# State-space scan and quantized feed-forward on one core: two additions of x begun behind the scan's last product, and a second early row quantized by DVE

## Chip, cores and metric

The kernel runs on one core of a Trainium2 chip (trn2). The metric is the device time of one execution in microseconds (us). Engines: PE multiplies matrices, DVE, ACT and POOL work on vectors, SP only issues DMAs here. POOL issues DMAs too; they run on a queue of their own, q0 (software), those of SP on q1 (hardware).

## What is computed

Cut to what matters, with the inputs x (4, 512, 512) and ctx (4, 512, 256):

```
z = layernorm(x)
u = silu(causal_conv(in_proj(ctx)) + conv_b);  B, C, dt = x_proj(u);  delta = softplus(dt_proj(dt) + b)
for each time step t:  state = state * exp(delta_t * A) + delta_t * u_t * B_t
                       y_t = sum over the 16 state columns n of state[:, n] * C_t[n]
x = x + (y + D * u) * silu(z)
h = silu(bit_linear(layernorm(x), w_gate)) * bit_linear(layernorm(x), w_up)
x = x + bit_linear(rms_norm(h) * ln_w, w_down)
```

bit_linear rounds its weights to −1, 0, 1 and each row of its input to 8 bits, with a scale from the row's largest magnitude.

## The kernel before

**Front.** Projections, convolution, softplus, the layernorm of x, its transpose and silu, the transpose of delta * u, and the rounding of the weights for gate and up (stored in HBM as w_ternary). All of x's memory on the chip (x_all, 16 rows of 128 x 512, four for each batch) then holds silu(z).

**Scan.** 64 steps, k = 16 * b + n, for batch b = 0 to 3 (a block of 16 steps each) and state column n. In a step ACT makes dB (L665, or a diagonal matrix, L662) and dA (four exponentials, L669), PE turns dB into four PSUM banks (L1182, or L1179 for the six columns of DIAG), DVE runs four scans of 128 x 512 (L882, which the profile lists as TENSOR_TENSOR_SCAN), POOL multiplies the four results by a row of C, laid over all partitions (L466, `product`), and PE adds the product up in four other PSUM banks, transposed (L1195, `add`; L1207 adds D * u in steps 4 to 7 of a block). PE's order is written out: in step k it turns dB for step k + 2, piece by piece between the four adds of product k − 1. The scans' results have a ring of four buffers (hs), so DVE may be three steps ahead of POOL. The rows of C come from HBM (c_rows) through SP's queue, one for each step (L334, `load_c`), each issued when the product two steps earlier is done, since c_bc has two buffers. After a batch's last step DVE multiplies its sum with silu(z) (`gate_y`, L892, four of 128 x 512), two scans into the third step of the next block; for batch 3, behind the scan. `add_x(b)` (L474) then adds x itself: a DMA from HBM, issued by POOL, that adds 1 MB into the batch's four rows of x_all.

SP's queue also carries in the scan: the rounded weights for gate (block 1) and up (block 2), w_down's raw pieces and ln_w (block 3) (L261, L345).

**Early rows in block 3.** The feed-forward part works by tiles t = 0 to 15 of 128 rows. Tile t needs the rows' statistics on DVE (`variance`, `bias`, L898 to L915), the reciprocal root on POOL (`power`, L478), the normalization on ACT (`norm`, L650), the row's scale on DVE (`scale_row`), the rounding on ACT, and the last step, the subtraction of MAGIC and the limit to 127, to bf16: `q1(t)`, 128 x 512. Then SP turns it by a DMA transpose into q1T (`turn_q1`, L349), which PE reads. For tiles 0 to 2 (EARLY) this is done within the scan's last block; POOL does the last step for tiles 0 and 1 (L492, behind products 6 and 10 of the block), DVE that for tile 2 behind its last scan (`cut_x`, L953).

**Behind the scan.** DVE waits for POOL's product of step 62 and makes the last one itself in two halves (L988), then cut_x(2), gated_up(0, 0) (L970) and gate_y(3). PE: the adds of step 62, gate_and_up(0, 0), the adds of step 63, gate_and_up(0, 1), and from then on the units of eight matmuls gate_and_up(t, j) for j = 0 to 3 (L1229), each first one of a tile waiting for q1T of the tile, and `down` for tile t − 2 at j = 2 (L1236). Each unit runs through ACT's silu (L714), DVE's gated_up (L970) and POOL's weighing with ln_w (L500). DVE's first statistics of batch 1 (`variance(4)`) come in tile 1, between gated_up(1, 0) and gated_up(1, 1); they wait for add_x(1). Those of batch 2 come in tile 5 and those of batch 3 in tile 9.

Of the kernel before, what the change touches and what calls it, by code (L numbers as in the profile page):

```python
# [25 lines left out]
ALU = mybir.AluOpType  # L26
# [4 lines left out]
NB, L, E = 4, 512, 512  # L31
# [13 lines left out]
MAGIC = 1.5 * 2.0 ** 23  # L45
# [22 lines left out]
def mixer_ffn(nc, x, ctx_t, in_t, conv_w, conv_b, xp_t, dt_t, dt_b, a_log, d_skip, w_all, ln_w, out):  # L68
    es = ExitStack()
    with es:  # L70
# [3 lines left out]
        def sem(name):  # L74
            return es.enter_context(nc.semaphore(name))
# [11 lines left out]
        def gate_rows(b):  # L87
            return x_all[:, b * KL:(b + 1) * KL, :]
# [94 lines left out]
        S = {n: sem(n) for n in names}  # L183
# [18 lines left out]
        def hold(eng, *waits):  # L202

            for name, v in zip(waits[0::2], waits[1::2]):
                if v > 0:
                    eng.wait_ge(S[name] if isinstance(name, str) else name, v)
# [33 lines left out]
        def xn(t):  # L240
            return xn_early[:, t, :] if t < EARLY else xn_late[:, t % 2, :]

        def q1(t):
            return (q1_early if t < EARLY else q1_late)[:, t % EARLY, :]

        def added(k, half):

            if k % DS == DS - 1 and half == 1:
                return "y_done", (k // DS + 1) * KL
            return "p_added", k * 2 + half + 1 - k // DS  # L250
# [8 lines left out]
        def _(sp):  # L259
            def load(dst, src, s):  # L260
                sp.dma_start(dst, src).then_inc(S[s], 16)  # L261
# [69 lines left out]
            def load_c(k):  # L331
                s, n = k % 2, k // 2
                hold(sp, "p_ready", k - 1)
                sp.dma_start(c_bc[:, s, :], c_dram[k // DS, k % DS, :].partition_broadcast(P)  # L334
                             ).then_inc(c_loaded[s], 16)
# [4 lines left out]
            def load_ternary(dst, w, k, s):  # L340
                sp.wait_ge(wq_stored[w][k], 16)
                load(dst[:, k, :], wq_dram[w * 4 + k, :, :], s)

            def load_down(k):
                sp.dma_start(w_full(WD_AT[k]), w_all[8 + k, :, :]).then_inc(wd_loaded[k], 16)  # L345

            def turn_q1(t):
                sp.wait_ge(S["q1_ready"], t + 1)
                sp.dma_start(q1T[:, t, :, :], q1(t), transpose=True).then_inc(q1T_done[t], 16)  # L349
# [7 lines left out]
            for b in range(NB):  # L357
                for n in range(DS):
                    if b * DS + n > 1:
                        load_c(b * DS + n)  # L360
                    if n >= 4 and n % 2 == 0 and n < 12 and b > 0:
                        k = n // 2 - 2
                        sp.wait_ge(S["y_gated"], b * KL)
                        if b == 1:
                            load_ternary(wg, 0, k, "wg_loaded")
                        if b == 2:
                            load_ternary(wu, 1, k, "wu_loaded")
                        if b == 3 and k < 2:
                            load_down(k)
                        if b == 3 and k == 2:  # L370
                            load(lnw, ln_w.partition_broadcast(P), "lnw_loaded")
                    if b == 3 and n == 12:
                        hold(sp, *added(b * DS + 8, 0))
                        load_down(3)
                    if b == 3 and n in (9, 13):
                        turn_q1(n // 4 - 2)
            sp.wait_ge(S["dA_ready"], NB * DS * KE)
            load_down(2)

            def store_out(t):  # L380
# [3 lines left out]
                    sp.wait_ge(S["fin_done"], t + 1)  # L384
                sp.dma_start(out_v[:, t, :], o_s[:, t % 2, :]).then_inc(out_stored[t % 2], 16)

            turn_q1(2)
            for t in range(TILES + 3):
                if tile(t - 3):
# [10 lines left out]
        def _(pool):  # L400
# [61 lines left out]
            def product(k):  # L462
                s = k % 2
                pool.wait_ge(c_loaded[s], (k // 2 + 1) * 16)
                pool.wait_ge(S["scan_done"], k * KE + KE)
                nc.gpsimd.tensor_tensor(hs[:, k % RING, :, :], hs[:, k % RING, :, :],  # L466
                                        c_bc[:, s:s + 1, :].to_broadcast([P, KE, L]),
                                        ALU.mult).then_inc(S["p_ready"], 1)
# [3 lines left out]
            def add_x(b):  # L472
                pool.wait_ge(S["y_gated"], (b + 1) * KL)
                nc.gpsimd.dma_start(gate_rows(b), x_v[:, b, :, :], accum_op=ALU.add).then_inc(x1_added[b], 16)  # L474

            def power(n, first, last):
                hold(pool, "var_ready", n)
                nc.gpsimd.tensor_tensor(rstd2[:, first:last], var2[:, first:last], mhalf[:, first:last],  # L478
                                        ALU.pow).then_inc(S["rstd_ready"], 1)

            for b in range(NB):
                for n in range(DS):
                    if b * DS + n < LAST:
                        product(b * DS + n)
                    if n == 3 and b > 0:
                        add_x(b - 1)
                    if b == NB - 1 and n % 4 == 0 and n // 4 < EARLY:
                        power(n // 4 + 1, 0, 1)
                    if b == NB - 1 and n in (6, 10):
                        t = n // 4 - 1  # L490
                        pool.wait_ge(S["x_rounded"], t + 1)
                        nc.gpsimd.tensor_scalar(q1(t), xn(t), MAGIC, 127.0, ALU.subtract,  # L492
                                                ALU.min).then_inc(S["q1_ready"], 1)
            add_x(NB - 1)

            def weigh(t, s, half):

# [271 lines left out]
        def _(dve):  # L769
# [179 lines left out]
            def cut_x(t):  # L949
                dve.wait_ge(S["x_rounded"], t + 1)  # L950
                if t >= 2 * EARLY:
                    dve.wait_ge(q1T_done[t - EARLY], 16)
                nc.vector.tensor_scalar(q1(t), xn(t), MAGIC, 127.0, ALU.subtract, ALU.min).then_inc(S["q1_ready"], 1)  # L953
# [13 lines left out]
            def gated_up(t, j):  # L967
                dve.wait_ge(S["sg_ready"], t * 4 + j + 1)
                dve.wait_ge(S["u_psum"], t * 4 + j + 1)
                nc.vector.tensor_tensor(h2[:, t % 2, j * 512:(j + 1) * 512], sg[:, j % 2, :], ps[:, U_BANK[(t * 4 + j) % 3], :],  # L970
                                        ALU.mult).then_inc(S["h_ready"], 1)

            for b in range(NB):
                for n in range(DS):
                    scan(b * DS + n)
                    t = n // 4
# [9 lines left out]
            for half in range(2):  # L986
                rows = slice(2 * half, 2 * half + 2)
                nc.vector.tensor_tensor(hs[:, LAST % RING, rows, :], hs[:, LAST % RING, rows, :],  # L988
                                        c_bc[:, LAST % 2:LAST % 2 + 1, :].to_broadcast([P, 2, L]),
                                        ALU.mult).then_inc(S["p_last"], 1)  # L990
            cut_x(2)
            gated_up(0, 0)
            gate_y(NB - 1)
# [315 lines left out]
```

## Time and profile before

| | us |
|---|---|
| median of three runs | 599.01 (597.3 to 599.84) |
| profiled execution, its own time | 597.98 |
| span of its trace | 596.2 |
| PE busy | 543.2 (91%) |
| DVE busy | 538.6 (90%) |
| ACT busy | 516.2 (87%) |
| POOL busy | 464.3 (78%) |

The span runs from the first instruction's start to the last one's end. Busy times are unions over each engine's instructions; waiting and the issuing of DMAs by SP are not counted. The scan's steps lie between about 100 and 414 us of the span, the feed-forward part behind them. In the timelines a row merges neighbouring instructions of one line: start, length, engine, line, operation, operands, how many, and in brackets how long the engine idled ahead of it and who ended that.

### The profile page before, as it was taken

To read this page: it belongs to the slowest core of one execution; us is meant where nothing else is said; L and a number is where in the kernel's file an instruction comes from. 1 tells how busy PE (TensorE), PEld (TensorE's weight loads), DVE (VectorE), ACT (ScalarE), POOL (GpSimd) and SP (SyncE) were. 2 spreads that over 40 slices of the span, in tenths; PEclk is the share of its full clock that TensorE was granted. 3 is DMA by queue.
4 is the path that set the end of the run, shared out by engine and by line. 5 is a ranking of instruction groups with operands and counts; after the bars stand their busy time and mean duration, and the time that the engine had idled before them with its cause. 6 is when DMAs were issued, how large, how long until landed. Compare 5 with 4: busy or idle time off the path is not lost.

```text
span 596.2 us, 10170 instructions
## 1 busy us (share of the span) xinstructions
PE 543.2 (91%) x3613; PEld 404.8 (68%) x3630; DVE 538.6 (90%) x814; ACT 516.2 (87%) x754; POOL 464.3 (78%) x182
## 2 busy tenths in 40 slices
PE   5977975799999999999899889998988999998996
PEld 2422565799998999989899889987333444443442
DVE  2999676999999999999999999998899999999874
ACT  2998698999999999989999798999877778867774
POOL 3574784799998999999899999994666565665662
PEclk9996788999999999999999899999999999999999
DMA  8993462111221652115531166243444342534421
GB/s 295 410 366 104 152 233 85 31 59 54 58 68 55 130 153 90 54 62 129 151 103 56 54 159 197 96 128 103 72 88 81 78 108 62 107 80 83 100 58 53
DMA packets 63185, 68.63 MB, mean 115 GB/s; under 512 B 42144, under 2 KB 42144, under 8 KB 60960
## 3 DMA queue, kind: packets, MB, share of 16 engines
q1 hardware_dynamic: 60832, 63.63, 36.0%
q0 software_dynamic: 2304, 4.36, 4.4%
q8 instruction: 29, 0.48, 0.3%
q14 instruction: 20, 0.16, 0.1%
HBM read 50.02 MB, written 8.52 MB: 98 GB/s over the span
## 4 chain that ended last, share of the span: by engine, by line
PE 27%; DVE 23%; ACT 21%; POOL 12%; issue 10%; DMA 6%; SPq 0%; DVEq 0%; ACTq 0%; POOLq 0%
POOL arena L466 11%; ACT arena L669 9%; ACT arena L665 7%; PE ps L1195 6%; DVE arena L792 5%; PE ps L1179 5%; PE ps L1229 4%; PE ps L1236 3%; PE ps L1182 3%; DVE arena L882 3%; DVE arena L970 2%; PE ps L1095 2%; DMA arena<-arena 2%; DMA arena<-c_rows 2%; ACT arena L662 2%
## 5 line engine op out<-in xcount | busy, mean ns | idle before, releaser
L466 POOL TENSOR_TENSOR arena<-arena 128x2048 f32<-128x2048 f32 x63 | 286.7, 4606 | 18.0 <-DVE arena L882 15.0
L882 DVE TENSOR_TENSOR_SCAN arena<-arena,ps 128x512 f32<-128x512 f32 x256 | 287.3, 1197 | 7.0 <-PE ps L1182 4.3
L669 ACT ACTIVATE arena<-arena,a_neg 128x512 f32<-128x512 f32 x256 | 165.1, 710 | 9.0 <-DVE arena L882 8.9
L1195 PE MATMUL ps<-ident,arena 128*128 128x128 f32 x1024 | 155.9, 276 | 7.0 <-POOL arena L466 3.8
L1195 PEld LDWEIGHTS ps<-ident,arena 128*128 128x128 f32 x1024 | 120.7, 142 | 11.2 <-POOL arena L466 7.0
L500 POOL TENSOR_TENSOR arena<-arena 128x1024 f32<-128x1024 f32 x30 | 71.1, 2372 | 58.2 <-DVE arena L970 58.2
L1229 PE MATMUL ps<-arena 128*128 128x512 bf16 x504 | 112.9, 379 | 2.1 <-DVE arena L970 1.1
L1182 PE MATMUL ps<-ident,arena 128*128 128x128 f32 x640 | 98.4, 279 | 10.1 <-ACT arena L665 7.8
L1179 PE MATMUL ps<-arena 128*128 128x128 f32 x768 | 103.4, 279 | 2.4 <-ACT arena L665 2.3
L665 ACT ACTIVATE arena<-arena,bT 128x512 f32<-128x512 f32 x160 | 101.9, 708 | 4.0 <-DVE a_neg L872 2.6
L1179 PEld LDWEIGHTS ps<-arena 128*128 128x128 f32 x768 | 94.9, 195 | 4.0 <-ACT arena L665 2.5
L1229 PEld LDWEIGHTS ps<-arena 128*128 128x128 bf16 x512 | 49.9, 98 | 62.4 <-DVE arena L970 2.1
L1182 PEld LDWEIGHTS ps<-ident,arena 128*128 128x128 f32 x640 | 76.2, 144 | 13.3 <-issue 8.5
L1236 PE MATMUL ps<-arena 128*128 128x512 bf16 x247 | 57.1, 379 | 8.1 <-DMA arena<-arena 5.5
L741 ACT ACTIVATE arena<-arena,magic,aq 128x2048 f32<-128x2048 f32 x15 | 31.4, 2093 | 29.5 <-DVE aq L931 29.4
L1236 PEld LDWEIGHTS ps<-arena 128*128 128x128 bf16 x256 | 24.3, 98 | 39.3 <-DMA arena<-arena 9.5
L714 ACT ACTIVATE arena<-ps,scales 128x512 f32<-128x512 f32 x64 | 42.6, 680 | 7.3 <-PE ps L1229 7.2
L970 DVE TENSOR_TENSOR arena<-arena,ps 128x512 f32<-128x512 f32 x64 | 43.5, 679 | 3.6 <-PE ps L1229 3.1
L1069 PE MATMUL ps<-arena 128*128 128x512 f32 x64 | 30.7, 638 | 9.8 <-DMA arena<-in_t 6.6
L957 DVE TENSOR_REDUCE half_max<-arena 128x1 f32<-128x1024 f32 x30 | 36.5, 1216 | 2.3
L436 POOL TENSOR_SCALAR arena<-arena,mv_x,rstd_x 128x512 f32<-128x512 f32 x16 | 34.0, 2132 | 0.4
L792 DVE SCALAR_TENSOR_TENSOR arena<-ps,cw,arena 128x511 f32<-128x511 f32 (+2 forms) x48 | 31.7, 736 | 0.0
(116 smaller groups left out, 576.5 us busy)
## 6 DMA issues: line engine op xcount, KB each, us to landing
arena<-w_all SPq DMA_DIRECT2D x16, 1024.0 KB, 9.4
arena<-c_rows SPq DMA_DIRECT2D x64, 256.0 KB, 3.3
arena<-x SPq DMA_DIRECT2D x4, 1024.0 KB, 18.0
w_ternary<-arena SPq DMA_DIRECT2D x8, 512.0 KB, 3.5
arena<-w_ternary SPq DMA_DIRECT2D x8, 512.0 KB, 5.1
arena<-x POOLq DMA_DIRECT2D x4, 1024.0 KB, 9.9
out<-arena SPq DMA_DIRECT2D x16, 256.0 KB, 2.0
arena<-ctx_t SPq DMA_DIRECT2D x4, 512.0 KB, 12.2
```

What stands on the lines that cost most here:

```text
L466: nc.gpsimd.tensor_tensor(hs[:, k % RING, :, :], hs[:, k % RING, :, :], c_bc[:, s:s + 1, :].to_broadcast([P, KE, L]), ALU.mult).then_inc(S ...
L500: nc.gpsimd.tensor_tensor(p2[:, s, w], h2[:, s, w], lnw[:, w], ALU.mult).then_inc(S["p2_ready"], 1)
L665: nc.scalar.activation(dB[:, slot(k), i, :], turned[:, b, i, :], ACT.Copy, scale=bT[:, b, i, n:n + 1]).then_inc(S["dB_ready"], 1)
L669: nc.scalar.activation(dA[:, s, i, :], delta_u[:, b, 0, i, :], ACT.Exp, scale=a_neg[:, i, n:n + 1]).then_inc(S["dA_ready"], 1)
L792: nc.vector.scalar_tensor_tensor(out=v[:, k, i:], in0=two("conv", b, h)[:, j, 0:L - i], scalar=cw[:, k, TAPS - 1 - i:TAPS - i], in1=v[:, k ...
L882: nc.vector.tensor_tensor_scan(out=hs[:, k % RING, i, :], data0=dA[:, k % 2, i, :], data1=ps[:, 4 + i, :], initial=0.0, op0=ALU.mult, op1= ...
L970: nc.vector.tensor_tensor(h2[:, t % 2, j * 512:(j + 1) * 512], sg[:, j % 2, :], ps[:, U_BANK[(t * 4 + j) % 3], :], ALU.mult).then_inc(S["h ...
L1179: last = mm(to, turned[:, k // DS, c, i * P:(i + 1) * P], dgB[:, slot(k), c, :], start=True, stop=True)
L1182: last = nc.tensor.transpose(to, dB[:, slot(k), c, i * P:(i + 1) * P], ident[:])
L1195: last = mm(ps[:, c, i * P:(i + 1) * P], hs[:, k % RING, i, c * P:(c + 1) * P], ident[:], start=(n == 0 and i == 0), stop=(n == DS - 1), i ...
L1229: last = mm(ps[:, bank, :], q1T[:, t, c, :], w[:, c, j * 512:(j + 1) * 512], start=(c == 0), stop=(c == KE - 1))
L1236: last = mm(ps[:, DOWN_BANK[t % 2], :], q2T[:, t % 2, c, :], wd(c), start=(c == 0), stop=(c == KI - 1))
```

## The change

Additions: add_x(0) stays in the scan, behind product 3 of block 1. add_x(1), add_x(2) and add_x(3) are issued by POOL one after the other behind its last product; before, the first two stood behind product 3 of blocks 2 and 3. Tile 1's last step of quantization goes from POOL (behind product 10 of block 3) to DVE (behind the last product, ahead of tile 2's). The DMA transpose of tile 1 goes in SP's list from behind the row of C of step 61 to the place behind the load of w_down's last piece, ahead of tile 2's.

```diff
@@ SP
-                    if b == 3 and n in (9, 13):
-                        turn_q1(n // 4 - 2)
+                    if b == 3 and n == 9:
+                        turn_q1(0)
             sp.wait_ge(S["dA_ready"], NB * DS * KE)
             load_down(2)
@@
+            turn_q1(1)
             turn_q1(2)
             for t in range(TILES + 3):
@@ POOL
-                    if n == 3 and b > 0:
-                        add_x(b - 1)
+                    if n == 3 and b == 1:
+                        add_x(0)
                     if b == NB - 1 and n % 4 == 0 and n // 4 < EARLY:
                         power(n // 4 + 1, 0, 1)
-                    if b == NB - 1 and n in (6, 10):
-                        t = n // 4 - 1
-                        pool.wait_ge(S["x_rounded"], t + 1)
-                        nc.gpsimd.tensor_scalar(q1(t), xn(t), MAGIC, 127.0, ALU.subtract,
+                    if b == NB - 1 and n == 6:
+                        pool.wait_ge(S["x_rounded"], 1)
+                        nc.gpsimd.tensor_scalar(q1(0), xn(0), MAGIC, 127.0, ALU.subtract,
                                                 ALU.min).then_inc(S["q1_ready"], 1)
-            add_x(NB - 1)
+            for b in range(1, NB):
+                add_x(b)
@@ DVE
+            cut_x(1)
             cut_x(2)
             gated_up(0, 0)
             gate_y(NB - 1)
```

POOL's list from block 3 of the scan (the products are L466 before, L467 in the changed file; the additions are the DMAs) to the first weighing of the feed-forward part, before:

```order
L466 TENSOR_TENSOR arena<-arena 128x2048 x3
L474 DMA arena<-x 128x4x512
L466 TENSOR_TENSOR arena<-arena 128x2048
L478 TENSOR_TENSOR rstd<-var,mhalf 128x1
L466 TENSOR_TENSOR arena<-arena 128x2048 x2
L492 TENSOR_SCALAR arena<-arena 128x512
L466 TENSOR_TENSOR arena<-arena 128x2048 x2
L478 TENSOR_TENSOR rstd<-var,mhalf 128x1
L466 TENSOR_TENSOR arena<-arena 128x2048 x2
L492 TENSOR_SCALAR arena<-arena 128x512
L466 TENSOR_TENSOR arena<-arena 128x2048 x4
L474 DMA arena<-x 128x4x512
```

and now:

```order
L467 TENSOR_TENSOR arena<-arena 128x2048 x4
L479 TENSOR_TENSOR rstd<-var,mhalf 128x1
L467 TENSOR_TENSOR arena<-arena 128x2048 x2
L492 TENSOR_SCALAR arena<-arena 128x512
L467 TENSOR_TENSOR arena<-arena 128x2048 x2
L479 TENSOR_TENSOR rstd<-var,mhalf 128x1
L467 TENSOR_TENSOR arena<-arena 128x2048 x6
L475 DMA arena<-x 128x4x512 x3
```

Three additions stand together behind the last product, one of the two quantizations of POOL is gone, and six products follow each other at the end.

SP's list at the end of the scan (rows of C L334, w_down's pieces L345, the transposes to q1T L349, the first one to q2T L354), before:

```order
L345 DMA arena<-w_all 128x2048
L334 DMA arena<-c_rows 128x512
L349 DMA_TRANSPOSE arena<-arena 128x4x128
L334 DMA arena<-c_rows 128x512 x2
L345 DMA arena<-w_all 128x2048
L349 DMA_TRANSPOSE arena<-arena 128x4x128
L354 DMA_TRANSPOSE arena<-arena 128x16x128
```

and now:

```order
L345 DMA arena<-w_all 128x2048
L334 DMA arena<-c_rows 128x512 x3
L345 DMA arena<-w_all 128x2048
L349 DMA_TRANSPOSE arena<-arena 128x4x128 x2
L354 DMA_TRANSPOSE arena<-arena 128x16x128
```

Tile 1's transpose now stands with tile 2's, behind the last rows of C and the last piece of w_down.

## Rows read from the trace of the kernel before

**Rows 1.** Windows: busy us of PE, PEld, DVE, ACT, POOL; clock, DMA share, GB/s.
```profile
190.00:265.00 75.00, 73.52 (x649) 71.23 (x648) 74.83 (x70) 72.65 (x131) 72.42 (x17) 1.00 0.37 99
265.00:340.00 75.00, 71.46 (x631) 69.31 (x629) 73.70 (x71) 71.28 (x128) 73.11 (x19) 1.00 0.37 99
...
479.40:490.00 10.60, 10.41 (x48) 4.81 (x50) 9.99 (x27) 8.38 (x10) 6.61 (x5) 1.00 0.39 88
```
**Rows 2.** Timeline of DVE, the scans of the second and the third block.
```profile
189.16 71.62 DVE L882 TENSOR_TENSOR_SCAN arena<-arena,ps 128x512 f32<-128x512 f32 x64
...
263.25 30.10 DVE L882 TENSOR_TENSOR_SCAN arena<-arena,ps 128x512 f32<-128x512 f32 x27
293.70 7.97 DVE L882 TENSOR_TENSOR_SCAN arena<-arena,ps 128x512 f32<-128x512 f32 x7 [0.35 <-PE ps L1182]
301.98 27.43 DVE L882 TENSOR_TENSOR_SCAN arena<-arena,ps 128x512 f32<-128x512 f32 x24 [0.30 <-PE ps L1179]
```
**Rows 3.** Timeline of POOL, second and third block.
```profile
212.09 63.43 POOL L466 TENSOR_TENSOR arena<-arena 128x2048 f32<-128x2048 f32 x14 [0.91 <-DMA arena<-c_rows]
275.43 1.24 POOL L474 DMA_DIRECT2D arena<-x  x1
276.27 9.49 POOL L466 TENSOR_TENSOR arena<-arena 128x2048 f32<-128x2048 f32 x2
287.66 49.76 POOL L466 TENSOR_TENSOR arena<-arena 128x2048 f32<-128x2048 f32 x11 [1.89 <-DMA arena<-c_rows]
```
**Rows 4.** What PE waited for, 264 to 330 us.
```profile
PE ps L1195 <- POOL arena L466: 1.8, 1, 1.8
```
**Rows 5.** Timeline of DVE, the scan's end and tiles 0 and 1.
```profile
397.17 11.20 DVE L882 TENSOR_TENSOR_SCAN arena<-arena,ps 128x512 f32<-128x512 f32 x10
409.34 2.36 DVE L988 TENSOR_TENSOR arena<-arena 128x1024 f32<-128x1024 f32 x2 [0.98 <-POOL arena L466]
411.62 0.42 DVE L953 TENSOR_SCALAR arena<-arena 128x512 bf16<-128x512 f32 x1
413.12 0.69 DVE L970 TENSOR_TENSOR arena<-arena,ps 128x512 f32<-128x512 f32 x1 [1.08 <-PE ps L1229]
...
422.71 0.68 DVE L970 TENSOR_TENSOR arena<-arena,ps 128x512 f32<-128x512 f32 x1
423.30 0.69 DVE L898 BATCH_NORM_STATS2 bst<-arena 128x6 f32<-128x512 f32 x1
```
**Rows 6.** Timeline of POOL, the scan's end.
```profile
389.17 1.93 POOL L492 TENSOR_SCALAR arena<-arena 128x512 bf16<-128x512 f32 x1
391.18 18.09 POOL L466 TENSOR_TENSOR arena<-arena 128x2048 f32<-128x2048 f32 x4
417.25 1.34 POOL L474 DMA_DIRECT2D arena<-x  x1 [7.98 <-DVE arena L892]
```
**Rows 7.** The 15 loads of rows of C between 112 and 180 us.
```profile
DMA to landing us min/median/max: 3.0/3.2/3.4
```
**Rows 8.** The chain that ended last, 281 to 288 us.
```profile
281.28 6.31 DMA arena<-c_rows
```
**Rows 9.** DMA view of 205 to 209 us: queues, and what SP issued.
```profile
q0 software_dynamic: 365, 0.75, 105.6%
...
arena<-c_rows SPq DMA_DIRECT2D x1, 256.0 KB, 5.3
```
**Rows 10.** The four additions, from issue to landing.
```profile
DMA to landing us min/median/max: 9.0/9.9/11.8
```
**Rows 11.** SP's transpose of tile 2, and how long it took to land.
```profile
412.07 1.20 SPq L349 DMA_TRANSPOSE arena<-arena  x1
...
DMA to landing us min/median/max: 2.4/2.4/2.4
```
**Rows 12.** Timeline of PE, units from gate_and_up(0, 2) on.
```profile
417.01 12.26 PE L1229 MATMUL ps<-arena 128*128 128x512 bf16 x55 [0.52 <-DVE arena L892]
```
**Rows 13.** DMA queues, 6.5 to 10.5 us, at the kernel's start.
```profile
q1 hardware_dynamic: 500, 1.22, 92.6%
q0 software_dynamic: 169, 0.16, 14.9%
```

## The prediction

> **What bounds the kernel now.** I read the timeline of DVE first, then POOL's, then the waits of PE, and last the DMA views, because the change moves transfers and hardly any arithmetic.
>
> Within the scan three engines are full: over 75 us of the second block PE is busy 73.5 us, DVE 74.8 and POOL 72.4 [rows 1]. DVE sets the pace. Where nothing disturbs it, ten scans take 11.20 us [rows 5]: the next begins 1.112 us after the last, and one step (four scans) takes 4.45 us. POOL's product takes about 4.53 us a step (14 in 63.43 us [rows 3]), so POOL drifts behind DVE by 0.08 us a step, which costs nothing until PE, which adds a product only when POOL has made it, comes too late with DVE's next input. DVE's timeline shows where that happens. From 263.25 to 329.41 (the end of the last piece, 301.98 + 27.43) it runs 58 scans; at 1.112 each and with the 0.08 us by which a scan outlasts its slot that is 64.6 us, and it took 66.2: **1.6 us lost**, the visible waits being for PE [rows 2]. The second block (64 scans in 71.62 us) lost only 0.4 by the same sum.
>
> Why there? POOL issues batch 1's addition at 275.43 (1.24 us of POOL), its next two products take 9.49 us (two undisturbed ones 9.06), and then POOL idles 1.89 us for a row of C that a DMA brings [rows 3]. PE in turn waits 1.8 us for POOL's product, the only wait of PE that this view lists [rows 4]. The row of C took 6.3 us from issue to landing, where 15 earlier ones took 3.0 to 3.4 [rows 7, 8]. The DMA view of 205 to 209 us, the same place one block earlier, says why: the software queue q0, which carries the addition, moves 365 packets at a share of 105.6%, and SP's queue q1 not one, though a row of C was issued at that time [rows 9]. **An addition, once at full rate, keeps SP's transfers out altogether.** This is the reading on which both the gain and the loss below rest.
>
> **The change part by part**, against the profiled execution (span 596.2, time 597.98; the median of the three runs is 599.01, 1.03 above it; I put the difference on the median).
>
> *Addition of batch 1 out of the third block.* Removes from POOL about 1.24 us of issue and slowed products, and the 1.89 us wait. PE then has its product some 3 us earlier and the 1.6 us of DVE should go. Below, 0 (PE is itself busy 71.5 of 75 us in the third block [rows 1] and might stall DVE anyway); above, 1.6. The second block, where POOL lagged less, lost 0.4, so I take 1.6 as the third's gain: with no addition at all it should lag less than the second did. What is late next is DVE itself.
>
> *Addition of batch 2 out of the fourth block.* Nothing: DVE there carries the rows' statistics besides its scans, so POOL catches up with it at every chain of them.
>
> *POOL's quantization of row 1.* 1.93 us off POOL, four products ahead of the end. POOL's last product ends at 409.27 (391.18 + 18.09) [rows 6] and DVE idles 0.98 us for it before its own last product [rows 5]. The scans of that product's step ended at 403.92 (408.37 less four slots); a product that starts 0.2 after that and takes 4.57 ends at 408.7. Gain 0.6; bounds 0 and 0.98. Both gains: **2.2 us**.
>
> *cut_x(1) on DVE.* 0.42 us more [rows 5], ahead of an idle time of 1.08 us that PE ends. Hidden; without that cover 0.42.
>
> *Two more issues on POOL behind its last product.* POOL idled 7.98 us there for DVE's gate [rows 6], so 2.6 us of issuing is hidden, and the addition of batch 3 is still issued 8.0 us after the last product (417.25). Variance(4), DVE's first reader of batch 1, comes 14.0 us after the last product (423.30 [rows 5]); additions landed after 9.0 to 11.8 us [rows 10], so it doesn't wait.
>
> *What these issues do to SP's queue.* Before, the transpose of row 2 went out at 412.07 into idle DMA engines and landed in 2.4 us [rows 11]; row 1's had been done in the scan. Now rows 1 and 2 are both turned there. I count from POOL's last product (409.27 before). The transpose of row 1 goes out at +2.8, as row 2's did. The addition of batch 1, issued at 0, is by then at full rate and batch 2's is queued behind it. PE needs row 1 at +11.2: its run of seven units from 417.01 takes 12.26 us, 1.75 each, and row 1 is the third [rows 12]. Its landing isn't in the trace, so I bound it. Below: as before, 2.4 after issue, +5.2, no loss. Above: behind all three additions. One lands 9.0 after its issue at best [rows 10]; each further one adds its bytes at the rate of [rows 9], 1.05 MB (four tiles of 128 x 512 floats) at 0.75 MB in 4 us, 5.6 us. So the three end at +9.0, +14.6 and +20.2, and a transfer that was kept out lands 0.4 us or a little more after (C's row at 281.28 + 6.31 = 287.59, its addition at 275.43 + 11.8 = 287.2 [rows 3, 8, 10]). I take **the middle case**, order of arrival: the first two additions are issued at 0 and +1.3, ahead of the transpose (+2.8), the third at +8, behind it. So row 1 lands behind the second, +15.2. PE is then 4.0 us late. DVE's product of row 1 started 0.45 us after PE's unit ended (422.71 against 420.51 + 1.75), so 3.5 us reach DVE. Behind it wait everything of DVE's list, variance(4) among it, ACT's silu(1, 0) and POOL's weighing of row 1; the feed-forward part then runs at DVE's pace (busy 9.99 of 10.6 us of a tile, PE 10.41 [rows 1]), so nothing is made good. Row 2 is needed six units in, at +18.2, now +22.2, and even behind the third addition (+20.8) it is in time.
>
> Sum: −2.2 + 3.5 = +1.3: **600.3 us**.
>
> **The rivals.**
>
> *1. SP's transposes get a turn between the additions.* For it: an addition is one transfer of its own, so the lock-out may hold for one only; in the kernel's first microseconds the two queues shared the engines well, q0 14.9% beside q1 92.6% [rows 13]. Against it: the full lock-out of [rows 9], with no second addition queued. Row 1 then lands at about +9.6 (9.0 and the same 0.6 as above), within the 11.2. Time 599.01 − 2.2 = **596.8 us**. The Trainium skill (DMA: Bandwidth & Descriptors, "Queues, rings and completion order") says that a DMA engine takes turns between its queues packet by packet, a packet having 9 to 17 descriptors as a rule and at most 64. By that rule this rival is what happens; the trace agrees with it at the start and not within one addition.
>
> *2. They wait for all three.* The engines stay with q0 as long as it has work, and the third addition, issued at +8, is queued before the second ends (+14.6). Row 1 lands at +20.8, PE is 9.6 late, DVE 9.1: +6.9 net, **605.9 us**, slower. It decides as soon as q0 is never empty from 0 to +20. For it: not a packet of q1 in the four microseconds of [rows 9]; against: no trace of two additions in a row.
>
> *3. The change doesn't give what it says:* the third block's stall is PE's own load (71.5 of 75 us [rows 1]) and stays, and only 0.6 is gained. With the forecast's loss, **601.9 us**.
>
> **How the numbers follow.** Forecast 0.34, rival 1 0.27, rival 2 0.22, rival 3 0.08, and 0.09 for what I don't see, half each way. A measurement of this kernel can tell about 0.5%, 3 us: under 596.0 or over 602.0. Faster: a quarter of rival 1 and half the rest, 0.11. Slower: rival 2, half of rival 3, a fifth of the forecast, half the rest, 0.36. Same: 0.53. The range goes from a little under rival 1 to a little over rival 2, 595.6 to 606.8. The likeliest case's own range is 599 to 602.
>
> **What would show it.** The timeline of DVE in the third block: 58 scans in under 65 us instead of 66.2, and no wait of POOL for C; else the first gain is wrong. DVE's idle time before its last product: 0.4 or less instead of 0.98. The landing of row 1's transpose: 7 us after issue for rival 1, about 12 for the forecast, 18 for rival 2; and a wait of PE for a DMA before its third unit of the feed-forward part, none, 4 or 9.6 us. If DVE waits for an addition ahead of variance(4), the forecast is wrong in a way I have not priced.

## The result and the profile after

| | before | changed |
|---|---|---|
| median, us | 598.15 | 605.38 |
| lowest to highest, 6 runs each | 596.02 to 599.84 | 601.4 to 607.67 |
| profiled execution: time (span), us | 597.98 (596.2) | 607.67 (605.9) |
| mean granted TensorE clock in it | 0.968 | 0.961 |

The ratio on record, which is worked out from all six runs of each and differs a little from the quotient of the medians, is 1.0116, with a 95% interval of 1.0089 to 1.0143: slower, by 7.2 us between the medians. The profiled execution is the slowest of the six; its extra 9.7 us of span hold 1.46 us that were lost before the second block began (190.62 against 189.16), in a part that the change doesn't touch.

**The gain came as forecast.** DVE and then POOL in the changed kernel, second and third block (columns as in [rows 2] and [rows 3]):

```profile
190.62 71.59 DVE L883 TENSOR_TENSOR_SCAN arena<-arena,ps 128x512 f32<-128x512 f32 x64
262.27 2.48 DVE L893 TENSOR_TENSOR arena<-ps,arena 128x512 f32<-128x512 f32 x4
264.67 64.54 DVE L883 TENSOR_TENSOR_SCAN arena<-arena,ps 128x512 f32<-128x512 f32 x58
```
```profile
202.09 1.41 POOL L475 DMA_DIRECT2D arena<-x  x1
203.02 9.61 POOL L467 TENSOR_TENSOR arena<-arena 128x2048 f32<-128x2048 f32 x2
213.46 122.22 POOL L467 TENSOR_TENSOR arena<-arena 128x2048 f32<-128x2048 f32 x27 [0.82 <-DMA arena<-c_rows]
```

The third block's 58 scans took 64.54 us in one stretch where they took 66.16 [rows 2], and POOL made 27 products without a gap where it had waited 1.89 us for C [rows 3].

**At the scan's end** DVE, then PE (compare [rows 5] and [rows 12]):

```profile
394.71 13.44 DVE L883 TENSOR_TENSOR_SCAN arena<-arena,ps 128x512 f32<-128x512 f32 x12 [0.24 <-ACT arena L670]
409.19 2.36 DVE L989 TENSOR_TENSOR arena<-arena 128x1024 f32<-128x1024 f32 x2 [1.03 <-DMA arena<-c_rows]
411.46 0.76 DVE L954 TENSOR_SCALAR arena<-arena 128x512 bf16<-128x512 f32 x2
412.34 0.69 DVE L971 TENSOR_TENSOR arena<-arena,ps 128x512 f32<-128x512 f32 x1
...
420.69 1.22 DVE L958 TENSOR_REDUCE half_max<-arena 128x1 f32<-128x1024 f32 x1
431.47 0.69 DVE L971 TENSOR_TENSOR arena<-arena,ps 128x512 f32<-128x512 f32 x1 [9.55 <-PE ps L1231]
...
439.73 1.23 DVE L1020 TENSOR_SCALAR arena<-arena 128x2048 bf16<-128x2048 f32 x1 [0.84 <-ACT arena L742]
```
```profile
408.54 1.97 PE L1197 MATMUL ps<-ident,arena 128*128 128x128 f32 x16 [0.71 <-POOL arena L467]
...
416.23 3.63 PE L1231 MATMUL ps<-arena 128*128 128x512 bf16 x16 [0.53 <-DVE arena L893]
427.77 13.38 PE L1231 MATMUL ps<-arena 128*128 128x512 bf16 x48 [7.91 <-DMA arena<-arena]
```

Up to 420.69 everything is ahead of before: there DVE's maximum of row 0 began at 421.57, so 0.88 us are gained in spite of the 1.46 lost at the front, 2.3 in all. Then PE, two units into its run of seven, stops for 7.91 us for a DMA, and DVE's product of row 1 begins at 431.47 instead of 422.71 [rows 5]. The loss at this place is 8.76 + 0.88 = **9.64 us**. Nothing is made good behind it, and 0.9 us more is lost before the tile is through, where DVE waits 0.84 us for ACT's rounding (439.73): the first transpose of the feed-forward part proper goes out at 440.99 instead of 431.35, 9.64 us late, and the last one 9.71 us. The sum for the profiled execution is 1.46 − 2.3 + 9.6 + 0.9 = 9.7 us, its whole difference of span. Without the front's 1.46 it is 8.2, beside 7.2 of the medians (5.3 to 8.6 by the interval).

**What the DMA was.** SP's queue, and the source view of POOL's additions and of SP's transposes:

```profile
404.00 0.32 SPq L334 DMA_DIRECT2D arena<-c_rows  x1
404.37 0.43 SPq L345 DMA_DIRECT2D arena<-w_all  x1
411.91 4.43 SPq L349 DMA_TRANSPOSE arena<-arena  x2
440.99 1.84 SPq L354 DMA_TRANSPOSE arena<-arena  x1
```
```profile
L475 POOL DMA_DIRECT2D arena<-x x3: 1283/1335/1775, 408.4 to 416.5; - x3
DMA to landing us min/median/max: 9.9/15.8/18.2
```
```profile
L349 SPq DMA_TRANSPOSE arena<-arena x3: 1777/1780/2610, 411.9 to 442.9; - x3
DMA to landing us min/median/max: 3.0/15.7/15.8
```

In order of issue: addition 1 at 408.42 landed at 418.29; addition 2 at 409.30, landed 425.13; the transposes of tiles 1 and 2 at 411.91 and 413.73 landed at 427.72 and 429.42; addition 3 at 416.47, landed 434.65. POOL's last product ended at 408.49, so the transpose of tile 1 landed at **+19.2**, where +11.2 was needed and +15.2 forecast.

Two DMA views of the changed kernel show how the queues shared the engines meanwhile (columns: packets, MB, share of 16 engines). A packet of these views is called a record here. From 411.5 to 415.5 us, with a transpose issued at 411.91:

```profile
q0 software_dynamic: 381, 0.78, 109.2%
```

and from 414 to 430 us:

```profile
q0 software_dynamic: 1320, 2.61, 93.0%
q1 hardware_dynamic: 1088, 0.26, 14.4%
```

In the first, SP's queue q1 isn't listed: it moved nothing, as in [rows 9]. In the second it moved 1088 records, both transposes, among 1320 of q0. Taken in bins of 0.5 us the records show three phases: up to 415.9, while the first addition drains, q0 alone; from 416 to 428 about as many records of q1 as of q0, some 45 each; then what is left. A data record of q0 is 2 KB and takes 178 ns, one of q1 256 bytes and 32 ns. One for one, the transposes' 545 records each pass only as fast as 545 of q0's do, some 6 us, though by itself such a transpose takes 2.4 us [rows 11].

That explains a landing near 422.5 to 424.4, and not the whole of it. Each DMA here signals its end in 16 parts, and the trace has their times. Of tile 1's transpose 15 parts came between 423.02 and 424.42 (+15.9), and the last one only at **427.72**, 3.3 us later. PE waits for the last. Of the third addition, too, 15 parts came from 429.00 to 429.75 and the last at 434.65.

**The clock.** Windows of the changed kernel around the wait (columns as in [rows 1]):

```profile
416.00:424.00 8.00, 3.63 (x16) 1.49 (x16) 4.52 (x9) 3.52 (x4) 6.53 (x4) 0.96 1.17 192
424.00:434.00 10.00, 6.23 (x16) 2.24 (x17) 2.32 (x7) 3.26 (x4) 0.48 (x1) 0.52 0.59 99
434.00:442.00 8.00, 7.20 (x35) 3.09 (x33) 6.77 (x20) 6.86 (x7) 2.61 (x3) 1.00 0.00 0
```

PE ran to 419.86, idled, and from 423.32 had the 1.2 GHz level for 10.2 us, so it came back to work with half the clock. Its first unit took 3.6 us, not 1.75: of the 9.64 lost, 7.9 are the wait itself, and the rest is this.

### The profile page after: what moved, and what is told of

Same layout as the page of the kernel before. It is cut to its first block, busy times and chain, and to the rows that moved or that the text cites. A ratio compares the mean times of both kernels' runs of the same rounds, so it can differ in the third digit from the quotient of the medians.

```text
span 605.9 us, 10187 instructions
## 1 busy us (share of the span) xinstructions
PE 547.0 (90%) x3630; PEld 404.9 (67%) x3630; DVE 539.4 (89%) x815; ACT 515.9 (85%) x754; POOL 462.4 (76%) x181
## 4 chain that ended last, share of the span: by engine, by line
PE 37%; DVE 24%; ACT 17%; issue 8%; DMA 8%; POOL 5%; SPq 0%; DVEq 0%; ACTq 0%; POOLq 0%
PE ps L1197 9%; ACT arena L670 8%; PE ps L1181 7%; PE ps L1231 6%; PE ps L1184 5%; ACT arena L666 5%; DVE arena L793 5%; DMA arena<-arena 5%; DVE arena L883 5%; POOL arena L467 4%; PE ps L1238 4%; DVE arena L971 2%; PE ps L1097 2%; DMA arena<-c_rows 2%; DMA arena<-x 1%
## 5 line engine op out<-in xcount | busy, mean ns | idle before, releaser
L467 POOL TENSOR_TENSOR arena<-arena 128x2048 f32<-128x2048 f32 x63 | 286.0, 4589 | 20.6 <-DVE arena L883 18.4
L1231 PE MATMUL ps<-arena 128*128 128x512 bf16 x512 | 116.5, 386 | 9.2 <-DMA arena<-arena 7.9
L1238 PE MATMUL ps<-arena 128*128 128x512 bf16 x256 | 58.0, 379 | 7.3 <-DMA arena<-arena 5.3
```

The lines of the kernel that those rows point to most:

```text
L1231: last = mm(ps[:, bank, :], q1T[:, t, c, :], w[:, c, j * 512:(j + 1) * 512], start=(c == 0), stop=(c == KE - 1))
L1238: last = mm(ps[:, DOWN_BANK[t % 2], :], q2T[:, t % 2, c, :], wd(c), start=(c == 0), stop=(c == KI - 1))
```

## The experiments

All were run against the kernel before, in two sets; its medians were 597.35 (31 runs) and 597.29 (24 runs). The ratios are those on record; where the effect is small they lie up to 0.15% below the quotients of the medians, so the sizes of the small gains are known no better than that. The edits are shown against the changed kernel. "+x" is microseconds after POOL's last product, which to 0.1 us is when its first addition there is issued.

**additions_only: the three additions moved, row 1 left with POOL and turned in the scan.**

```
-                    if b == 3 and n == 9:
-                        turn_q1(0)
+                    if b == 3 and n in (9, 13):
+                        turn_q1(n // 4 - 2)
...
-            turn_q1(1)
...
-                    if b == NB - 1 and n == 6:
+                    if b == NB - 1 and n in (6, 10):
...
-            cut_x(1)
```

> Theory A: the loss is tile 1's transpose, which waits on SP's queue behind the additions. Here the three additions stand behind the last product as in the change, but tile 1 is quantized by POOL and turned within the scan as before. The third block of the scan gains the 1.6 us, tile 1 finds its rows turned, and only tile 2's transpose goes beside the additions; it lands 15 to 19 us after POOL's last product and is needed at +18.2. So 0 to 1 us of loss and 1.5 to 2.2 of gain: 596 to 598 against 598.15. Theory B: the loss lies in the additions themselves (x of batch 1 late for variance(4), or POOL busy with descriptors). Then nothing of the 7 us goes: about 605, and DVE idles ahead of variance(4).

Measured 596.16 (594.83 to 598.63, 10 runs), ratio 0.9975 (0.9949 to 1.0002). PE's run of seven units is unbroken:

```profile
416.64 12.26 PE L1230 MATMUL ps<-arena 128*128 128x512 bf16 x55 [0.53 <-DVE arena L893]
```

The third block's 58 scans took 64.55 us. The additions still queued up (408.82 to 418.77, 409.71 to 424.43, 416.88 to 430.24), and tile 2's transpose, issued at 412.44, took 11.4 us, landing at +15.0, but it is needed only at +18:

```profile
DMA to landing us min/median/max: 11.4/11.4/11.4
```

So the additions by themselves cost nothing there; what costs is that a transpose is needed early behind them.

**row1_only: row 1 on DVE and turned behind the scan; the additions as before.**

```
-                    if n == 3 and b == 1:
-                        add_x(0)
+                    if n == 3 and b > 0:
+                        add_x(b - 1)
...
-            for b in range(1, NB):
-                add_x(b)
+            add_x(NB - 1)
```

> The other half alone: additions as before, tile 1 quantized by DVE behind the scan and turned there. Theory A: both transposes go into idle DMA engines and land within 6 us of POOL's last product, 5 us before PE needs the first. The 0.6 us at the scan's end stay, the third block keeps its stall: 597.0 to 598.2. Theory C: two transposes in a row on SP's queue, each issued in 1.8 to 2.6 us, are slow by themselves; then PE waits for tile 1 here too and the time is 601 or more.

Measured 597.99 (596.36 to 599.08), ratio 0.9999 (0.9972 to 1.0026). Both transposes went through idle engines, the first from 413.18 to 416.71 in 3.52 us, the second in 2.72, and PE waited for none. DVE's second quantization costs nothing, and neither half of the change is slow: **only the two together are**. The 0.6 us that this half should gain is too small to be told here.

**one_behind: batch 2's addition stays in the fourth block, batch 1's goes behind the last product.**

```
-                    if n == 3 and b == 1:
-                        add_x(0)
+                    if n == 3 and b in (1, 3):
+                        add_x(b - 1)
...
-            for b in range(1, NB):
-                add_x(b)
+            add_x(1)
+            add_x(NB - 1)
```

> As the change, but batch 2's addition stays in the scan's last block as before; only batch 1's stands behind the last product, and batch 3's follows at +8 as in both kernels. Theory A: tile 1's transpose waits for one addition and lands at +9.5 to +11, in time for PE at +11.2; the whole gain of 2.2 us shows: 595.5 to 597.5. If a single addition already makes it late, PE waits 1 to 3 us and the time is 597 to 599.

Measured **595.82** (594.12 to 597.64, 10 runs), ratio 0.9959 (0.9935 to 0.9983): the lowest median of all, 1.5 us under its set's kernel before by the medians and 2.4 by the ratio, though not told apart from in_block3 or additions_only. With a single addition ahead (407.58 to 417.40) tile 1's transpose was kept until it was nearly through and landed at 417.86, +10.3, within the +11.2:

```profile
410.99 3.88 SPq L349 DMA_TRANSPOSE arena<-arena  x2
```
```profile
415.38 12.26 PE L1231 MATMUL ps<-arena 128*128 128x512 bf16 x55 [0.53 <-DVE arena L893]
```

So it is the second addition, queued right behind the first, that makes tile 1 late.

**in_block3: batch 1's addition behind product 8 of the fourth block, batch 2's behind product 3.**

```
-                    if n == 3 and b == 1:
-                        add_x(0)
+                    if n == 3 and b in (1, 3):
+                        add_x(b - 1)
+                    if n == 8 and b == 3:
+                        add_x(1)
...
-            for b in range(1, NB):
-                add_x(b)
+            add_x(NB - 1)
```

> As the change, but batch 1's addition is issued in the scan's last block behind product 8, and batch 2's stays behind product 3 of it. DVE has its chains of small operations there, so POOL's lag should be made good and a late row of C be absorbed. Theory A: transposes in 6 us, no wait of PE, the third block without its stall: 595.5 to 597. If the additions stall the last block as they did the third, it is 597.5 to 598.5, with POOL waiting for a row of C around step 59 and DVE's scans stretched.

Measured 596.12 (594.82 to 598.0), ratio 0.9973 (0.9947 to 0.9999); the transposes took 2.45 and 2.78 us. POOL has room for two additions in the fourth block, as the part on batch 2's addition assumed. Its last product is then the last thing that DVE waits for, as before the change:

```profile
407.64 2.36 DVE L990 TENSOR_TENSOR arena<-arena 128x1024 f32<-128x1024 f32 x2 [1.28 <-POOL arena L467]
```

**third_later: the changed kernel with batch 3's addition moved to the end of tile 1**, so that nothing is queued behind the first two.

```
-            for b in range(1, NB):
+            for b in range(1, NB - 1):
                 add_x(b)
...
+                    if t == 1:
+                        add_x(NB - 1)
```

> As the change, but batch 3's addition is issued at the end of tile 1 instead of at +8 from POOL's last product, so only two additions are queued ahead of or beside the transposes. In the changed kernel's trace tile 1's transpose shared the DMA engines packet by packet with the second and third addition. If the third matters, tile 1 lands at +14 to +16 and the time is 600 to 602; if the second alone already costs everything (alternation from +8 to +14 carries all 545 packets but for a slow engine), it lands at +18 to +19.5 and the time stays at 604 to 606.

Measured 603.38 (601.55 to 605.22, 3 runs), ratio 1.0102 (1.0071 to 1.0132). Both transposes landed with the end of the second addition (425.21), at 425.23 and 425.62, +15.4, and PE waited 4.10 us:

```profile
425.27 0.60 PE L1233 MATMUL ps<-arena 128*128 128x512 bf16 x2 [4.10 <-DMA arena<-arena]
```
```profile
L349 SPq DMA_TRANSPOSE arena<-arena x2: 1347/1712/2076, 412.9 to 414.3; - x2
DMA to landing us min/median/max: 11.3/11.8/12.3
```

These are the forecast's own numbers, +15.2 and 4.0, in a kernel in which the third addition isn't there. Whether the third addition is what costs the other 3.8 us of the changed kernel's wait is **not shown**, and much speaks against it. The two times can't be told apart (1.0102 and 1.0116). In additions_only the third addition was issued at +8.1 beside a transpose that still landed at +15.0. And in the changed kernel itself 15 of the 16 parts of tile 1's transpose had landed by +15.9. What sets the two profiled executions apart is the last of the 16 parts, 3.3 us behind the fifteenth there and 0.01 us here. DVE lost more than the 3.5 us that the forecast gave this case: the product of row 1 follows its predecessor by 7.20 us (421.28 to 428.48) instead of 1.96 (420.75 to 422.71 before), 5.2 lost, since here too PE had the 1.2 GHz level, for 3.4 us from 425.81, half a microsecond after it came back. −2.2 + 5.2 is +3.0, while the median is +6.1 (+4.2 to +7.9 by its interval). In the profiled execution the rest has a place: 2.6 us at the front (the second block began at 191.78) and 1.3 at the end. Whether three runs fell high or the edit costs more, they don't say.

**second_after_rows: the second addition only after SP has been told of all rows**, the transposes issued ahead of it.

```
-            for b in range(1, NB):
-                add_x(b)
+            add_x(1)
+            pool.wait_ge(S["q1_ready"], EARLY)
+            add_x(2)
+            add_x(3)
```

> As the change, but POOL issues the second and third addition only when DVE has quantized tiles 1 and 2 (+3.2 from its last product), just behind SP's issue of tile 1's transpose (+2.8). Theory of my forecast (order of arrival): that transpose is then ahead of the second addition and lands right behind the first, at +9.5 to +10.5; no loss for tile 1, 596 to 598. Theory of alternation (once SP's queue has got in, the two queues take turns packet by packet, whoever came first): nothing changes against the changed kernel, tile 1 lands at +15 or later and the time is 602 to 606.

Measured 596.47 (594.67 to 599.54, 8 runs), ratio 0.9984 (0.9965 to 1.0003). SP's and POOL's queues:

```profile
412.27 3.65 SPq L349 DMA_TRANSPOSE arena<-arena  x2
```
```profile
409.13 1.38 POOL L475 DMA_DIRECT2D arena<-x  x1
412.88 1.28 POOL L475 DMA_DIRECT2D arena<-x  x1 [2.37 <-DVE arena L956]
417.19 1.28 POOL L475 DMA_DIRECT2D arena<-x  x1 [3.03 <-DVE arena L895]
```

Tile 1's transpose was issued 0.6 us ahead of the second addition and landed at 419.25, +10.1, just behind the first one's end (418.87). Tile 2's, issued at 413.60, took 12.98 us and landed at +17.4. PE's run is unbroken. With the same three additions, the second 2.9 us later than in the changed kernel, tile 1 lands 9.1 us earlier, and the ratio to before is 0.9984 instead of 1.0116: **when the second addition is issued decides**. Whether that is by its order behind the transpose or by its distance from the first addition, this run changes together and doesn't tell; in the trace q1 had 310 records in the half microsecond from 417.5, as the first addition ran out, while q0 had 25.

**rows_first: all three additions wait until both transposes have landed.**

```
+            for t in range(1, EARLY):
+                pool.wait_ge(q1T_done[t], 16)
             for b in range(1, NB):
                 add_x(b)
```

> As the change, but POOL issues the additions only when both transposes have landed, at about +6.5. The transposes are then as fast as in row1_only, and the price moves to the additions: batch 1's lands at +15.5 to +17 instead of +9, variance(4) wants it at +14, so DVE idles 1.5 to 3 us there and the time is 597.5 to 599.5. If the lock-out were not the cause, PE would still wait for tile 1.

Measured 600.77 (599.2 to 601.33, 6 runs), ratio 1.0055 (1.0032 to 1.0078), dearer than expected. The transposes took 3.29 us and less; the price moved to POOL and DVE:

```profile
415.63 3.98 POOL L475 DMA_DIRECT2D arena<-x  x3 [7.35 <-issue]
418.03 2.16 POOL L479 TENSOR_TENSOR rstd<-var,mhalf 128x1 f32<-128x1 f32 x1
```
```profile
420.23 0.21 DVE L918 TENSOR_SCALAR bia<-mv,rstd 128x1 f32<-128x1 f32 x1 [2.35 <-POOL rstd L479]
422.55 1.22 DVE L960 TENSOR_REDUCE half_max<-arena 128x1 f32<-128x1024 f32 x1 [0.92 <-POOL arena L503]
424.59 0.69 DVE L901 BATCH_NORM_STATS2 bst<-arena 128x6 f32<-128x512 f32 x1 [0.23 <-DMA arena<-x]
```

Three issues in a row stand ahead of the power that DVE needs, and variance(4) waits for its x, a wait that no other kernel here has.

**gate_first: only one addition behind the last product, the other two after the gate.**

```
-            for b in range(1, NB):
-                add_x(b)
+            add_x(1)
+            pool.wait_ge(S["y_gated"], NB * KL)
+            add_x(2)
+            add_x(3)
```

> As the change, but the second and third addition both wait for DVE's last gate (+8). The queue is empty of further additions when the first ends (+8.5 to +9), so the transposes land at +9.5 to +10.5 as in one_behind and PE doesn't wait. One more issue of 1.3 us stands ahead of POOL's power for row 4, whose result DVE waits for: up to 1.3 us of DVE's time. 596 to 597.5; 595.8 as one_behind if that issue is hidden. Were tile 1's wait a matter of POOL's issues and not of q0's content, PE would wait here too.

Measured 597.41 (596.46 to 598.96, 10 runs), ratio 0.9999 (0.9985 to 1.0013). Tile 1 landed at +10.0, and what was gained was given back by one more issue of POOL's at a place where DVE waits for it:

```profile
419.07 0.21 DVE L918 TENSOR_SCALAR bia<-mv,rstd 128x1 f32<-128x1 f32 x1 [1.61 <-POOL rstd L479]
```

## Why the prediction was right and wrong

The forecast was 600.3 us, in a range of 595.6 to 606.8. It was 605.38: within the range, near its upper end, and slower by more than the 0.5% that can be told, to which the text gave 0.36 (its own parts add up to 0.37). The likeliest case's own range, 599 to 602, missed it; the stated range holds it because it reached up to rival 2. The place and the kind of the loss were right, its size was not: 9.6 us, where 3.5 were counted.

- *1.6 us from the third block: right in this execution.* 64.54 us for 58 scans where 64.6 was worked out, and no wait for C. Every kernel without an addition there took 64.54 or 64.55; row1_only, which keeps it, took 65.27, so the stall that goes is 1.6 us in one execution and 0.7 in another: that it was 1.6 in the execution compared is in part luck.
- *0.6 us at the scan's end: right in size, wrong in its sign to look for.* DVE's idle time ahead of its own last product is 1.03 us, not 0.4: POOL is out of its way, and the last row of C, issued at 404.00 and landed at 409.10, took its place. In the kernel before that row had landed at 409.26, 0.01 us ahead of POOL's end: it was the wait hidden behind POOL. The 0.6 came through PE, whose last adds wait for POOL only and began 0.6 us earlier after the last scan than before.
- *Fourth block nothing, cut_x(1) hidden, variance(4) not waiting: right.* The two quantizations run together in 0.76 us, and gated_up(0, 0) follows them at once.
- *Issues on POOL: right* (2.66 us for two, the third at +7.98 for a forecast +8.0).
- *"The middle case, order of arrival": this is the step that failed.* It said that tile 1's transpose is kept out until the second addition is through and lands behind it, at +15.2, with PE 4.0 us late. It landed at +19.2 and PE waited 7.9. The lock-out of [rows 9] is real, but it holds only until the first addition runs out, to 7.5 us after its issue (415.93); then SP's queue gets about one record for each of POOL's. The transpose wasn't waiting behind the second addition but went slowly beside it, and 15 of its 16 parts had landed by 424.42, before the second addition's last (425.13). That this is +15.9, close to the forecast, is in part luck: 545 records at that pace take about as long as the rest of the second addition. The other part of the miss is the sixteenth part, 3.3 us behind; with it at 424.42 PE would have waited some 4.6 us (an estimate from 419.86). What held it up stays open. The reason that the forecast gave for leaving the third addition out, that it is issued later, isn't refuted by any run.
- *"3.5 us reach DVE": wrong by the clock.* The 9.64 us lost here are 7.9 of wait and the rest, some 1.8, for PE's first unit at half clock. The text counted a late start and an unchanged pace; in the records before, PE had no low stretch in this place. In third_later the same term came to 5.2.

Rival 2 named 605.9 us and came closest, with its landing at +20.8 for +19.2, by luck: its reason, that q1 gets nothing as long as q0 has work, is not what happened: from 416 to 428 q1 had its turns throughout. Rival 1's reason is the nearer one: the transposes did get turns between the additions, but turns so thin that they didn't help. The Trainium skill (DMA: Bandwidth & Descriptors, "Queues, rings and completion order") says that a DMA engine takes turns between its queues. The trace agrees from 416 us on and disagrees in the 4 us of the first addition, where q0 moved 381 packets and q1 none.

Left open: why the first addition shuts q1 out and the later ones don't; what held up the last part of tile 1's transpose, and whether it does so in every run; and how the clock's part varies from run to run. The median's 7.2 us is nearer to the profiled loss with the late part than without it, but only one execution was traced. The changed kernel's spread of 6.3 us (601.4 to 607.67) says nothing here: the kernel before, in 31 runs, spread over 7.2.

## What to carry to other kernels

Moving background transfers to where "the queue is idle" means looking for the small transfer that somebody needs soon behind them, and at which number of large ones it becomes late: here one addition ahead of the transpose was free (+10.3 for a needed +11.2) and two cost 9.6 us, 3.3 of it by a part of the transpose that came late for an unknown reason. A wait that held the second addition back by 2.9 us, to behind the transpose, repaired it. Where a wait is for a DMA, look at when its parts landed and not only at the last, before naming a cause. Two halves of an edit, each free alone, are to be tried together and apart. When a wait is removed, read what is the next to arrive (here a row of C) before counting its whole length; and for a stall of TensorE add the clock that it comes back with, about 1.8 us here on top of 7.9.

The version to keep is one_behind: the third block's gain without the queue, 595.82 us, 0.9959 (0.9935 to 0.9983) of the kernel before. in_block3 does as well, as far as can be told.

## What was not expected of the hardware

- Sharing goes by records and not by bytes: 1088 records of q1 with 0.26 MB took as long as 1320 of q0 with 2.61 MB. A transpose that took 2.4 us alone [rows 11] took 11.4 to 13.0 beside such records, and 15.8 with one part late.
- The queues' sharing has two modes in one stretch: none for q1 within the first addition, one for one afterwards. It was so in all ten traces, wherever something of SP's was issued 3 us or more after an addition that found q0 idle: q1's first record came when 387 to 491 of the addition's 512 data records had gone, 7.0 to 9.1 us after the addition's issue and 1.2 to 4.4 us after SP's. In second_after_rows q1 moved 67, 361 and 116 records in the three microseconds from 416 on, as the first addition ran out, though its transpose had been issued at 412.27.
- An addition of 1 MB with none ahead of it took 8.9 to 10.4 us behind the scan (9.82 in one_behind), and the second queued behind it ended 5.1 to 6.8 us after the first (14.60 against 9.94 us from issue in third_later); beside the transposes that 5.6 us a transfer of the forecast was about right for q0, and wrong for whoever stood beside it.
- The third addition landed 18.18 us after its issue in the changed kernel, and in its last 5 us the records thin out to 3 in 0.5 us, about what one DMA engine alone would move at 178 ns a record. Nothing waits for this addition. But the last part of tile 1's transpose had been late shortly before, and PE waited for that. In the other kernels' transposes there the last part came at most 1.1 us behind the fifteenth. That both are one lagging engine is likely and not shown; why it lags was not tried.
